# Segment sums in 64x64 products, paired first states and a pre-added square sum in a state-space loop

## The reference, cut to what matters

```python
CHUNK = 32                      # heads 64, head width 8, state width 128, d_in 512
dt = softplus(dt + dt_bias); A = -exp(A_log)
dA = (dt * A) in chunks;  dA_cum = cumsum(dA, axis=-1)
Lmat = exp(segsum(dA))          # segsum[t, s] = dA[s+1] + ... + dA[t]
Y_diag = einsum("bcthn,bcshn,bhcts,bcshp->bcthp", Ch, Bh, Lmat, x * dt)
decay_states = exp(dA_cum[..., -1:] - dA_cum)
states = einsum("bcshn,bhcs,bcshp->bchpn", Bh, decay_states, x * dt)
prev = (states carried over the chunks by their decays)
Y_off = einsum("bcthn,bchpn,bhct->bcthp", Ch, prev, exp(dA_cum))
y = Y_diag + Y_off + D * x
hg = y * silu(gate);  var = mean(hg * hg)
out = (hg * rsqrt(var + eps) * norm_w) @ out_proj_w.T;  x = x + out
```

## Time and profile before

| | us |
|---|---|
| three runs of the kernel, median | 692.53 |
| lowest and highest of them | 692.39, 693.21 |
| the profiled execution, its own time | 689.73 |
| span of the profiled execution | 687.9 |
| busy in the span: PE | 541.2 (79%) |
| busy in the span: DVE | 407.4 (59%) |
| busy in the span: ACT | 373.0 (54%) |
| busy in the span: POOL | 147.5 (21%) |
| mean granted TensorE clock, share of full speed | 0.905 |

### The profile page before, as it was taken

The page is one execution under the profiler, slowest core; times in us unless marked ns, Lnnn a source line. Parts: engine busy times, 40 slices in busy tenths (PEclk is TensorE's granted clock), DMA queues, the critical chain, the costliest instruction groups (busy, mean ns, idle before and its releaser), DMA issues.

```text
span 687.9 us, 13927 instructions
## 1 busy us (share of the span) xinstructions
PE 541.2 (79%) x5668; PEld 392.5 (57%) x5668; DVE 407.4 (59%) x612; ACT 373.0 (54%) x794; POOL 147.5 (21%) x115
## 2 busy tenths in 40 slices
PE   0097769778687766578999999999649999999980
PEld 0054445556455642353664656667648999996560
DVE  5889999999997477966655544454831111111223
ACT  6987788978876407555657555666322222222112
POOL 1000000000000127732019555520021222223110
PEclk9995699878868999899999999999759999999995
DMA  9500000000001000000000000000269999888825
GB/s 350 189 1 1 1 1 1 2 1 1 1 1 32 1 0 1 0 1 1 2 2 2 3 2 2 3 2 3 69 256 423 420 420 361 333 330 304 338 95 191
DMA packets 18480, 71.38 MB, mean 104 GB/s; under 512 B 4849, under 2 KB 9969, under 8 KB 14705
## 3 DMA queue, kind: packets, MB, share of 16 engines
q1 hardware_dynamic: 15408, 64.20, 24.5%
q0 software_dynamic: 1920, 5.25, 2.0%
q10 hardware_dynamic: 1088, 1.05, 0.5%
HBM read 65.77 MB, written 4.72 MB: 102 GB/s over the span
## 4 chain that ended last, share of the span: by engine, by line
PE 52%; DVE 31%; ACT 8%; issue 4%; DMA 3%; POOL 1%; SPq 0%; ACTq 0%; DVEq 0%; POOLq 0%
PE PS L1442 39%; DVE arena L942 4%; DVE nmx L1029 4%; DVE arena L939 4%; PE PS L1948 2%; PE PS L2017 2%; PE PS L1724 1%; PE PS L1589 1%; DVE R L956 1%; DVE arena L953 1%; DVE arena L954 1%; DMA arena<-in_moe 1%; DVE arena L948 1%; DVE arena L949 1%; ACT arena L773 1%
## 5 line engine op out<-in xcount | busy, mean ns | idle before, releaser
L1442 PE MATMUL PS<-arena 128*128 128x128 f32 (+6 forms) x1376 | 156.9, 291 | 17.6 <-DVE arena L1126 11.4
L1442 PEld LDWEIGHTS PS<-arena 128*128 128x128 f32 (+4 forms) x1376 | 125.8, 164 | 41.9 <-issue 25.0
L611 ACT ACTIVATE arena<-PS,nmx 128x128 f32<-128x128 f32 (+1 forms) x128 | 52.0, 422 | 32.6 <-DVE nmx L1029 32.6
L1390 DVE TENSOR_TENSOR R<-arena,PS 128x128 f32<-128x128 f32 x16 | 4.6, 288 | 88.1 <-ACT arena L870 88.1
L389 POOL TENSOR_SCALAR arena<-ident,gcol 128x128 f32<-128x128 f32 x4 | 2.4, 602 | 220.2 <-DMA gcol<-in_gcol 220.2
L449 POOL TENSOR_TENSOR arena<-arena 128x1024 f32<-128x1024 f32 x16 | 37.8, 2367 | 40.6 <-DVE arena L1208 32.5
L1506 PE MATMUL PS<-arena 32*128 32x128 f32 (+1 forms) x128 | 22.9, 438 | 29.9 <-ACT arena L611 29.6
L481 POOL DMA_INDIRECT ypair<-arena,oid x20 | 19.8, 988 | 121.8 <-ACT arena L876 121.8
L1442 PE MATMUL PS<-arena,R 128*128 128x256 f32 x192 | 44.2, 380 | 0.6 <-ACT arena L876 0.6
L1442 PEld LDWEIGHTS PS<-arena,R 128*128 128x128 f32 x192 | 35.2, 190 | 5.1 <-issue 1.0
L942 DVE TENSOR_TENSOR_SCAN arena<-dmat,arena 128x1023 f32<-128x1023 f32 x16 | 37.6, 2348 | 0.6
(11 more groups left out here) (306 smaller groups left out, 1198.3 us busy)
## 6 DMA issues: line engine op xcount, KB each, us to landing
arena<-in_moe SPq DMA_DIRECT2D x23, 1408.0 KB, 8.2
arena<-in_moe SPq DMA_DIRECT2D x23, 768.0 KB, 9.7
inproj<-in_inproj SPq DMA_DIRECT2D x1, 1344.0 KB, 10.5
arena<-in_fT SPq DMA_DIRECT2D x1, 1024.0 KB, 5.0
xT<-in_xT SPq DMA_DIRECT2D x1, 1024.0 KB, 5.4
R<-in_w1T SPq DMA_DIRECT2D x1, 1024.0 KB, 7.4
R<-in_w2T SPq DMA_DIRECT2D x1, 1024.0 KB, 9.4
R<-in_w3T SPq DMA_DIRECT2D x1, 1024.0 KB, 11.5
```

Of the source, the lines that this page charges most:

```text
L611: sc.activation(pr[u % 2][:, j, 0:n], PS[:, 2 * (u % 2) + j // 2, (j % 2) * 256:(j % 2) * 256 + n], ACT.Exp, bias=nmx[:, u % 2, j:j + 1], ...
L1442: last = mm(dst, l, r, start=(n == 0), stop=(n == len(pairs) - 1))
```

## The change

Segment sums: with 32-token chunks, `ugt` is block diagonal, so its two 64x64 halves on the diagonal hold all of it. A new buffer `dAq` holds `dA` with the heads dealt out by row halves and column halves; four copies on DVE fill it after the second slice of the convolution. Row half r and column half c of it hold the tokens of half c of the tile, for the heads of group r. POOL's steps reads `dAq`; `segments(i, j)` issues four products, 64x64 by 64x512, one for each r and c: product (r, c) reads rows 64r to 64r+63 and writes rows 64c to 64c+63 of bank r. One call with j = 0 and one with j = 1 stand where four calls stood; each call waits for both banks to be empty.

First states: B and the weighted inputs of state 1 are written to rows 64 to 95 (`btok0`, `xw`), while those of state 2 stay on rows 0 to 63. `first_states(i)` issues state 1 and state 2 one behind the other, into banks 4 and 5. PE's order becomes: segments 0 of i+1; tokens of i+1; first states of i; segments 1 of i+1; state 3 of i; state 4; the rest as it was. ACT's copies wait for both and are reordered likewise.

Squares: DVE adds the four quarters of `sqT` in one reduction (`square_sum`, into `sq1`), behind front(i+1) in its order, and PE issues one product with the ones matrix, now behind the eight of the out-projection. The semaphore dve_dtx is merged into dve_dt.

The diff, with the lines between cut to a few:

```diff
@@ -203,11 +203,14 @@
         dA = arena[:, 24 * K + 512:25 * K].rearrange("p (i h) -> p i h", i=NT)
+        dAq = arena[:, 29 * K + 384:29 * K + 896].rearrange("p (i c j n) -> p i c j n", i=NT, c=2, j=2)
         ddt = arena[:, 25 * K:27 * K].rearrange("p (c i h) -> p c i h", c=NC, i=NT)
 ...
         rsb, btok, gm = pair(28 * K + 768, P), pair(29 * K, P), pair(29 * K + 256, Q)
+        btok0 = [arena[:, 27 * K + 256 + P * i:27 * K + 256 + P * (i + 1)] for i in range(2)]
+        sq1 = [spent[:, 512 + 2 * K:640 + 2 * K], arena[:, 29 * K + 896:30 * K]]
         diag = ekvq[:, 0:XT * P].rearrange("p (k n) -> p k n", k=XT)
@@ -289,7 +292,7 @@
             act_sw dve_h act_ss3 pool_z3 dve_scale3 act_y3 dve_hq pe_hqt pe_o act_o pe_ot pe_gate act_gate pe_xbc
-            act_cv dve_cv act_xc pe_dt dve_dtx act_sp2 dve_dt pe_tok dve_tok pool_stp pe_seg act_seg pool_m pe_yd
+            act_cv dve_cv act_xc pe_dt dve_sq act_sp2 dve_dt pe_tok dve_tok pool_stp pe_seg act_seg pool_m pe_yd
             pe_yo dve_hg act_opw pe_op pe_lg dve_mask pe_rank dve_tab pe_xtok act_xtok pe_xbt act_xbt act_si dve_hb
@@ -437,8 +440,8 @@
                 if i >= 2:
-                    pool.wait_ge(S["pe_seg"], 4 * (i - 1))
-                pool.tensor_tensor(stp[i % 2], dA[:, i, :].unsqueeze(2).broadcast_to([P, SH, Q]),
+                    pool.wait_ge(S["pe_seg"], 2 * (i - 1))
+                pool.tensor_tensor(stp[i % 2], dAq[:, i].rearrange("p c j n -> p (c j n)").unsqueeze(2).broadcast_to([P, SH, Q]),
                                    step[:].unsqueeze(1).broadcast_to([P, SH, Q]), ALU.mult).then_inc(S["pool_stp"], 1)
@@ -452,7 +455,7 @@
             last.then_inc(S["pool_diag"], 1)
-            pool.wait_ge(S["dve_dt"], 1)
+            pool.wait_ge(S["dve_dt"], 3)
             steps(0)
@@ -703,7 +706,7 @@
 
-            act.wait_ge(S["dve_dtx"], 1)
+            act.wait_ge(S["dve_dt"], 1)
             soft = ut.rearrange("p (i h) -> p i h", i=NT)
@@ -751,7 +754,7 @@
 
-                act.wait_ge(S["pe_seg"], 4 * i + q + 1)
+                act.wait_ge(S["pe_seg"], 2 * i + q // 2 + 1)
                 if i >= 2 and q == 0:
@@ -759,7 +762,7 @@
 
-                act.wait_ge(S["pe_s"], SBEF[i] + c)
+                act.wait_ge(S["pe_s"], SBEF[i] + max(c, 2))
                 if i and c == 1:
@@ -795,14 +798,15 @@
             for i in range(NT):
-                state(i, 1)
                 if i + 1 < NT:
 ...
                     decays(i + 1, 1)
+                state(i, 1)
                 state(i, 2)
+                if i + 1 < NT:
+                    decays(i + 1, 2)
                 state(i, 3)
                 if i + 1 < NT:
-                    decays(i + 1, 2)
                     decays(i + 1, 3)
@@ -1173,7 +1177,7 @@
             done(v.tensor_tensor(dt, bank(0).rearrange("p (i h) -> p i h", i=NT),
-                                 dtb[:].unsqueeze(1).broadcast_to([P, NT, SH]), ALU.add), "dve_dtx")
+                                 dtb[:].unsqueeze(1).broadcast_to([P, NT, SH]), ALU.add), "dve_dt")
             dve.wait_ge(S["act_sp2"], 1)
@@ -1186,6 +1190,12 @@
                                                 o[:, :, back:], ALU.mult, ALU.add), "dve_cv" if back == 3 else "dve_self")
+                if n == 1:
+                    by_head = dA.rearrange("p i (j r n) -> p i j r n", j=2, r=2)
+                    for r in range(2):
+                        for c in range(2):
+                            done(v.tensor_copy(dAq[64 * r:64 * r + 64, :, c], by_head[64 * c:64 * c + 64, :, :, r, :]),
+                                 "dve_dt" if r and c else "dve_self")
                 if 1 <= n <= NC:
@@ -1205,13 +1215,15 @@
                 done(v.tensor_copy(btok[i % 2], bank(3, P)))
+                done(v.tensor_copy(btok0[i % 2][64:64 + Q, :], PS[0:Q, 3, 0:P]))
                 done(v.tensor_tensor(gm[i % 2], PS[:, 3, P:P + Q], step[:], ALU.mult), "dve_tok")
 ...
                     m = Q * c
-                    done(v.tensor_tensor(heads(xw[i % 2][0:m, c - 1, :]), heads(PS[0:m, 2, :]), per_head(ddt[0:m, c - 1, i, :], m),
+                    to = slice(64, 64 + Q) if c == 1 else slice(0, m)
+                    done(v.tensor_tensor(heads(xw[i % 2][to, c - 1, :]), heads(PS[0:m, 2, :]), per_head(ddt[0:m, c - 1, i, :], m),
                                          ALU.mult), "dve_xw" if c == 4 - i % 2 else "dve_self")
@@ -1248,6 +1260,12 @@
 
+            def square_sum(i):
+                dve.wait_ge(S["act_hgt"], i + 1)
+                if i >= 2:
+                    dve.wait_ge(S["pe_op"], i - 1)
+                done(v.tensor_reduce(sq1[i % 2], sqT[i % 2].rearrange("p (l n) -> p n l", l=XT), X, ALU.add), "dve_sq")
+
             dve.wait_ge(S["act_xc"], 6)
@@ -1258,6 +1276,8 @@
                     front(i + 1)
+                if i:
+                    square_sum(i - 1)
 
@@ -1271,6 +1291,7 @@
             add_out(NT - 2)
+            square_sum(NT - 1)
 
@@ -1727,7 +1748,7 @@
                 conv_in(n)
-            pe.wait_ge(S["dve_dt"], 1)
+            pe.wait_ge(S["dve_dt"], 2)
             for n in range(NC + 2):
@@ -1755,30 +1776,36 @@
 
-            def segments(i, q):
+            def segments(i, j):
 
                 pe.wait_ge(S["pool_stp"], i + 1)
-                if i == 0 and q < 2:
+                if i == 0 and j == 0:
                     pe.wait_ge(S["act_gate"], NT)
                 else:
-                    pe.wait_ge(S["act_seg"], 4 * i + q - 1)
-                acc(bank(q % 2), [(ugt[:], stp[i % 2][:, 16 * q:16 * q + 16, :].rearrange("p h t -> p (h t)"))], "pe_seg")
+                    pe.wait_ge(S["act_seg"], 4 * i + 2 * j)
+                for r in range(2):
+                    rows, cols = slice(64 * r, 64 * r + 64), [slice(64 * c, 64 * c + 64) for c in range(2)]
+                    for c in range(2):
+                        last = mm(PS[cols[c], r, :], ugt[rows, rows],
+                                  stp[i % 2][rows, 32 * c + 16 * j:32 * c + 16 * j + 16, :].rearrange("p h t -> p (h t)"), start=True, stop=True)
+                last.then_inc(S["pe_seg"], 1)
+
+            def first_states(i):
+
+                pe.wait_ge(S["dve_xw"], i + 1)
+                pe.wait_ge(S["dve_tok"], i + 1)
+                if i:
+                    pe.wait_ge(S["act_s"], SBEF[i - 1] + 3)
+                    if i % 2 == 0:
+                        pe.wait_ge(S["dve_hg"], i)
+                    else:
+                        pe.wait_ge(S["act_s"], SBEF[i])
+                acc(bank(4), [(btok0[i % 2][64:64 + Q, :], xw[i % 2][64:64 + Q, 0, :])], "pe_s")
+                acc(bank(5), [(btok[i % 2][0:2 * Q, :], xw[i % 2][0:2 * Q, 1, :])], "pe_s")
 
 ...
 
-                n = SBEF[i] + c - 1
-                if c == 1:
-                    pe.wait_ge(S["dve_xw"], i + 1)
-                    pe.wait_ge(S["dve_tok"], i + 1)
-                    if i:
-                        pe.wait_ge(S["act_s"], SBEF[i - 1] + 3)
-                elif c == 2:
-                    if i % 2 == 0 and i:
-                        pe.wait_ge(S["dve_hg"], i)
-                    elif i:
-                        pe.wait_ge(S["act_s"], SBEF[i])
-                else:
-                    pe.wait_ge(S["act_s"], SBEF[i] + c - 2)
+                pe.wait_ge(S["act_s"], SBEF[i] + c - 2)
                 m = Q * c
@@ -1830,27 +1857,24 @@
                     pe.wait_ge(S["act_opw"], XT)
-                acc(PS[:, 3, 0:P], [(ones[:], sqT[i % 2][:, l * P:(l + 1) * P]) for l in range(XT)])
                 for mt in range(CT):
-                    last = acc(PS[:, 3, 256 + mt * P:256 + (mt + 1) * P],
-                               [(outproj[:, l, mt * P:(mt + 1) * P], hgT[i % 2][:, l * P:(l + 1) * P]) for l in range(XT)])
-                last.then_inc(S["pe_op"], 1)
+                    acc(PS[:, 3, 256 + mt * P:256 + (mt + 1) * P],
+                        [(outproj[:, l, mt * P:(mt + 1) * P], hgT[i % 2][:, l * P:(l + 1) * P]) for l in range(XT)])
+                pe.wait_ge(S["dve_sq"], i + 1)
+                acc(PS[:, 3, 0:P], [(ones[:], sq1[i % 2])], "pe_op")
 
 ...
             tokens(0)
-            for q in range(4):
-                segments(0, q)
+            for j in range(2):
+                segments(0, j)
             for i in range(NT):
-                state(i, 1)
                 if i + 1 < NT:
                     segments(i + 1, 0)
+                    tokens(i + 1)
+                first_states(i)
+                if i + 1 < NT:
                     segments(i + 1, 1)
-                    tokens(i + 1)
-                state(i, 2)
                 state(i, 3)
-                if i + 1 < NT:
-                    segments(i + 1, 2)
-                    segments(i + 1, 3)
                 if i % 2 == 0:
 ...
                 within(i)

```

## The result

The changed kernel takes 703.87 us (median of 4 runs, 702.90 to 704.66), the kernel before 692.46 us in the same comparison: ratio 1.018, 95% interval 1.015 to 1.021, so 1.8% slower. The forecast was 692.7 with a range of 686 to 697.5. The profiled execution took 703.71 us against 689.73, its span 701.5 against 687.9: 13.6 us of span to explain.

What follows compares the result with a forecast made beforehand. PE, busy nearly throughout the state-space loop, bounds the kernel until the next ring of waits closes. 3.7 us gained less 3.9 lost in the tail gives +0.2: 689.9 profiled, 2.8 more for the median, 692.7; range 686 to 697.5.

Steps and rivals of the forecast that it cites:

- Segments: Segment sums on PE: four 64x64 products overlap fully, 1.0 us a call, taking 1.5 us a tile off PE.
- Rival 3: Segment products on PE overlap only in pairs, 0.9 us more a call: +8.8, 701 us; chance 0.06.
- States: The two first states on PE run one after the other because their shapes differ: 2.10 us, no gain.
- Squares: Three ones products leave PE, 0.66 us a tile; DVE gets a 512-element reduction of 0.69 us.
- rival 4: The strided reduction of squares on DVE takes 1.22 us: +3, 695.5 us; chance 0.06.
- The ring: Loop of waits through DVE, PE and ACT, per tile: 15.3 and 13.8 us, 29.1 a pair against 30.3.
- The first step for odd i: DVE's way to the tokens step: square_sum 0.69, gated 3.32, add_out 0.88 and handovers, 5.1 us.
- The ends: Outside the steady loop: 2.1 us gained before it, 0.4 lost in its first tile, 3.9 lost after it.
- The tail: From ACT's copies of turned tile 6 to the router's first operation: 9 us instead of 5.2, losing 3.9.
- My case: The main forecast: 692.7 us, range 691 to 694.5 for handovers and one fall of the clock; chance 0.36.
- the rival: New waits before PE's tokens bring 1.2 GHz; two or three falls, 3.4 to 5 us, 695.7 to 697.5; chance 0.18.
- step 2: PE's part of each tile: tokens, first states, segments, state three and the handover to ACT, 5.2 us.

Runs made afterwards that it cites:

- e5_padded: The changed kernel with state one padded by zeros to 64 rows, so both first states are 64x128 products; 686.89 us, ratio 0.995 to the kernel before.
- e1_filler: The changed kernel with sixteen useless PE transposes ahead of the wait for add_out before the tokens of tiles 3, 5 and 7; 693.50 us, ratio 1.005.
- e9_gates_first: The changed kernel with the two gate products on DVE ahead of the reduction of tile 6 instead of behind it; 702.26 us, ratio 1.017.
- e2_squares_back: The changed kernel without square_sum, the four ones products back on PE behind the out-projection; 690.62 us, ratio 1.003.

## Why the prediction was wrong

**Segments** (1.0 a call): right; 1.09 and full overlap. Rival 3 would have given 701, near the measured time, and is excluded by that row alone; the 1.98 of the odd tile is the same call at half the clock (granted 0.52), not rival 3's 1.9.

**States** (2.10, no gain): right, 2.11. The e5_padded row shows why: the shapes. The rule of the Trainium skill (TensorEngine Tiling (Array Packing), Key Properties), that a change of tiling mode drains the engine, agrees with this: 2.11 for two modes, 1.06 for one.

**Squares**: DVE's place in the ring was right, its price was not. The reduction of strided elements takes 1.06, not 0.69, nearer to rival 4's 1.22.

**The ring** (15.3 and 13.8): even tiles 13.97; odd ones, read from e1_filler where no fall lies in them, 15.64, 0.3 more than forecast, for which the reduction's extra 0.37 accounts. (The first step for odd i adds up to 5.0, not 5.1; the ring of 15.3 stands even so.) PE's waits before the tokens were 2.23 and 0.97 for a forecast of 1.9 and 1.0.

**The ends**: 2.4 sooner at H(0) (2.1 forecast). The tail lost 4.3 (3.9), and e9_gates_first confirms 2.0 of it for the gate products.

**The clock** is the step that failed. My case allowed for one fall at most, and the rival priced it with "Each fall doubles some 1.7 us of PE work". Three came in this profile, and a full one doubled nearly all of step 2, from tokens to states: 4.8 us, of which no slack before the output gives anything back. In the profiled execution the odd tiles exceed e1_filler's (15.66 for the first, 15.64) by 3.2, 4.8 and 4.7, together 12.7. Without them H(0) to H(6) would be 1.6 less than before, where the forecast had 1.7 less (2.1 gained, 0.4 lost), and the whole 703.71 less 12.7 = 691.0 against a forecast of 689.9 for that execution. That 1.6 and 1.7 agree is partly luck: the loss of 0.4 from H(0) to H(1) did not come (15.66 in e1_filler, 15.86 before), and neither did the gain of some 0.3 in each later odd tile (15.64 against 15.65). The rival had the mechanism and the right place, but I priced it too low, gave it 0.18 and let my range end inside it. Its argument against, that most of the new stretches keep PE busier than 1.43 of 3.40 us, did not hold for the odd tile: ahead of the tokens PE was busy for 1.12 of 3.35 us (419.40 to 422.75). I had the price from one short stretch; here the clock stayed down for nearly all of 10.7 us.

## What to carry to other kernels

Keeping an engine busy without a break can be worth more than shortening its work, since it may keep its clock: when a change shortens PE's work, look at once for the wait that opens up, price the work behind it at half the clock, and cover the wait with work that was due later anyway. Work taken off the bound engine pays only if the ring gets shorter by it and the ends do not get longer. The segments alone gave 10 us. The squares moved to DVE left the changed kernel's ring as it was (at full clock 14.0 and 15.6 a pair with them in e1_filler, 14.5 and 15.0 without in e2_squares_back), made the waits ahead of the tokens longer, and lengthened the tail by 4 to 5 us. The two first states, on separate rows of the array, overlapped only when both had one tile shape, and zeros were a cheap way to give them one.

## What was not expected of the hardware

Adding 48 transposes of no use made a kernel about 9 us faster. Falls of the clock followed waits of 0.86, 1.0 and 2.2 us in some places and not in others, so a wait's length alone does not tell whether one comes. The strided 512-element reduction took 1.06 us where one over 512 elements from PSUM took 0.69. Whether PE could start the tokens as soon as ACT has read the sum of squares, without DVE's add_out, was not tried: tokens and output use one bank of PSUM, and no other wait in this kernel keeps their accesses apart.
